# A graph layer's aggregation with the source rows stationary and the destinations moving

## The reference

```
gnn  = segment_sum((xn @ W)[src] * edge_weight, dst)       # 42500 edges
mix  = s * v / s, v = xn @ Wv.T + bv, s per head and row from exp maps of q and k
x1   = x + gnn + mix
r    = layernorm(x1)
out  = x1 + down(silu(gate(r)) * up(r))
```

## Time and profile before

| | |
|---|---|
| profiled execution | 1668.56 us |
| its span, first to last instruction | 1666.6 us |
| PE (matmul) busy | 1643.1 us, 99% |
| DVE busy | 1115.9 us, 67% |
| ACT busy | 487.1 us, 29% |
| POOL busy | 636.8 us, 38% |
| mean granted TensorE clock | 0.998 |
| moved by DMA | 302.89 MB |

### The profile page before, as it was taken

One profiled execution on the slowest core, in us unless ns is written; L12 is line 12 of the kernel. 1 busy time (PEld: TensorE's weight loads), 2 busy tenths in 40 slices (PEclk: granted clock), 3 DMA queues, 4 the chain that ended last, 5 costly groups with the idle time before them and its releaser, 6 DMA issues.

```text
span 1666.6 us, 22401 instructions
## 1 busy us (share of the span) xinstructions
PE 1643.1 (99%) x7896; PEld 1333.1 (80%) x7896; DVE 1115.9 (67%) x2568; ACT 487.1 (29%) x591; POOL 636.8 (38%) x497
## 2 busy tenths in 40 slices
PE   7999999999999999999999999999999999999998
PEld 6899999877777888887788878878777877777665
DVE  7866583576777766755555566676775674774885
ACT  4632311322111111123311023333333232332554
POOL 2011465777777777776688304410300000000000
PEclk9999999999999999999999999999999999999999
DMA  9999888765686755567866656555555345433554
GB/s 314 350 418 347 310 262 252 187 141 122 151 210 146 196 146 131 136 150 176 236 135 136 148 157 198 178 170 162 139 171 138 113 121 136 138 113 93 148 172 124
DMA packets 154777, 302.89 MB, mean 182 GB/s; under 512 B 61624, under 2 KB 92392, under 8 KB 154713
## 3 DMA queue, kind: packets, MB, share of 16 engines
q1 hardware_dynamic: 78469, 206.81, 39.5%
q0 software_dynamic: 66192, 62.07, 17.1%
q10 hardware_dynamic: 10052, 33.26, 6.6%
HBM read 202.88 MB, written 99.20 MB: 181 GB/s over the span
## 4 chain that ended last, share of the span: by engine, by line
PE 85%; DVE 7%; DMA 5%; SPq 1%; issue 1%; ACT 1%; DVEq 0%; ACTq 0%
PE PS L377 21%; PE PS L378 21%; PE PS L379 21%; PE PS L1543 5%; PE PS L1545 5%; PE PS L1544 5%; PE PS L1794 4%; DMA Aside<-A_dense 3%; PE PS L1824 2%; PE PS L1609 2%; DVE SL L1310 1%; DVE stats L1337 1%; DVE zr L1331 1%; DVE AL L1312 1%; DMA z<-zx 1%
## 5 line engine op out<-in xcount | busy, mean ns | idle before, releaser
L726 POOL DMA_INDIRECT A_dense<-wtot,cell x333 | 532.7, 1600 | 213.3 <-DMA A_dense<-wtot,cell 121.2
L377 PE MATMUL PS<-SL,AH 125*125 125x512 f32 x784 | 309.0, 394 | 3.5 <-DVE AL L1312 3.4
L378 PE MATMUL PS<-SH,AL 125*125 125x512 f32 x784 | 310.3, 396 | 0.0
L379 PE MATMUL PS<-SH,AH 125*125 125x512 f32 x784 | 310.1, 396 | 0.0
L377 PE MATMUL PS<-WL,xtH 128*125 128x512 f32 x640 | 251.9, 394 | 0.9 <-DVE xtL L1199 0.8
L378 PE MATMUL PS<-WH,xtL 128*125 128x512 f32 x640 | 251.5, 393 | 0.0
L379 PE MATMUL PS<-WH,xtH 128*125 128x512 f32 x640 | 251.3, 393 | 0.0
L1310 DVE TENSOR_TENSOR SL<-S,SH 125x1024 fp32r<-125x1024 f32 x98 | 119.6, 1221 | 137.6 <-ACT SH L954 137.6
L954 ACT ACTIVATE SH<-S 125x1024 fp32r<-125x1024 f32 (+1 forms) x98 | 104.1, 1062 | 346.1 <-PE PS L379 345.9
L377 PEld LDWEIGHTS PS<-SL,AH 125*125 125x125 f32 x784 | 145.8, 186 | 44.0 <-DVE AL L1312 6.8
L378 PEld LDWEIGHTS PS<-SH,AL 125*125 125x125 f32 x784 | 146.1, 186 | 36.3
(11 more groups left out here) (191 smaller groups left out, 2606.2 us busy)
## 6 DMA issues: line engine op xcount, KB each, us to landing
A_dense<-zeros POOLq DMA_DIRECT2D x40, 1280.0 KB
xt<-xnT SPq DMA_DIRECT2D x60, 500.0 KB
Araw<-A_dense SPq DMA_DIRECT2D x100, 250.0 KB, 2.7
Aside<-A_dense SPq DMA_DIRECT2D x100, 250.0 KB, 3.0
keyrow<-key_rows SPq DMA_DIRECT2D x42, 512.0 KB
ewrow<-weight_rows SPq DMA_DIRECT2D x42, 512.0 KB
xnT<-XT ACTq DMA_DIRECT2D x20, 500.0 KB, 8.2
zx<-in_x SPq DMA_DIRECT2D x20, 448.0 KB
```

Source lines behind the costliest of these rows:

```text
L377: nc.tensor.matmul(o, lh, rl, start=start, stop=False)
L378: nc.tensor.matmul(o, ll, rh, start=False, stop=False)
L379: return nc.tensor.matmul(o, lh, rh, start=False, stop=stop)
L726: pool.indirect_dma_start(cells[m], bass.IndirectOffsetOnAxis(cell[:, col:col + 1], 0), wtot[:, col:col + 1], None, compute_op=ALU.add).th ...
```

## The change

PE's operands in the aggregation change places. Before, 125 destinations of A were stationary and 512 features of S moved. After, a slice of 128 features of S is stationary and the group's 500 destinations move; PSUM holds features on partitions, one slice a bank. DVE no longer adds z: it transposes the banks in blocks of 32 x 32 into an SBUF tensor (`turn_sums`), and POOL adds that to z in device memory by accumulating DMAs (`add_sums`) and loads the sums back into zr (`rows_back`). So that a block row comes out contiguous, ACT writes S with its columns permuted (`sources_out`). r goes away; z takes its place. Statistics move to pairs 3 and 4, rounding to pairs 5 to 8, the last three weight chunks to pairs 1, 2 and 9 of group 1. In the feed-forward stage the last rows' statistics move to tiles 4 and 5, and their rounding to tiles 7, 9, 11 and 13.

```
-ROUNDED_AT = (4, 6, 9, 12)
+ROUNDED_AT = (7, 9, 11, 13)
+STATS_AT = 4
-CHUNK_OF = {(0, h): h - 1 for h in range(1, HALF)} | {(1, h): h + 2 for h in range(3 + GT, HALF)}
+CHUNK_OF = {(0, h): h - 1 for h in range(1, HALF)} | {(1, 1): 9, (1, 2): 10, (1, 9): 11}
+STATS_PAIR, QUANT_PAIR = 3, 5
+FULL_BLOCKS, LAST_ROWS = GN // 32, GN % 32
...
 PE
+        def by_slice(i, sh, sl, d, first, last_one):
+            for k in range(2 * d, 2 * d + 2):
+                cols = slice(k * P, (k + 1) * P)
+                last = product3(PS[:, k, 0:GN], sh[:, cols], sl[:, cols], AH[i][0:ROWS, :], AL[i][0:ROWS, :], first, last_one)
+            return last
...
-                rows = slice(d * ROWS, (d + 1) * ROWS)
-                for c in range(2):
-                    cols = slice(c * 512, (c + 1) * 512)
-                    last = product3(PS[0:ROWS, 2 * d + c, :], AH[i][0:ROWS, rows], AL[i][0:ROWS, rows],
-                                    sh[:, cols], sl[:, cols], first, last_one)
+                last = by_slice(i, sh, sl, d, first, last_one)
...
 DVE
-        def add_z(g):
-            dve.wait_ge(s_zin, 32 * GT + g * 32)
+        def turn_sums(g):
             for d in ORDER:
...
-                nc.vector.tensor_tensor(zr[0:ROWS, d, :], two_banks(d)[0:ROWS], zr[0:ROWS, d, :], ALU.add).then_inc(s_r[d], 1)
+                nc.vector.transpose(sums_of(g)[:, :, 64 * d:64 * d + 64].rearrange("p c (b i) -> p b c i", b=2),
+                                    PS[:, 2 * d:2 * d + 2, :].rearrange("p b (c j) -> p b c j", j=32)).then_inc(s_r[d], 1)
...
         def row_stats(g, tiles):
             for d in tiles:
-                dve.wait_ge(s_r[d], g + 1)
+                dve.wait_ge(s_back, g * (16 * GT) + 16 * (d + 1))
...
+        def group(g, chunks=False, at_end=False):
+            for h in range(HALF):
+                m = g * HALF + h
+                low_of_sources(2 * h, 0, m)
+                sum_of_blocks(1, m)
+                if h == 0:
+                    turn_sums(g - 1)
+                if h == QUANT_PAIR:
+                    inverse_deviation(g - 1)
+                d = h - QUANT_PAIR
+                if 0 <= d < GT:
+                    largest_r(g - 1, d)
...
+                low_of_sources(2 * h + 1, 1, m)
+                if not at_end or h + 1 < HALF:
+                    sum_of_blocks(0, m + 1)
+                if h in (STATS_PAIR, STATS_PAIR + 1):
+                    row_stats(g - 1, ((0, 1), (2, 3))[h - STATS_PAIR])
+                if h == STATS_PAIR + 1:
+                    row_moments(g - 1)
+                if 0 <= d < GT:
+                    round_r(g - 1, d)
...
 DVE, feed-forward stage
-        add_z(GROUPS - 1)
-        row_stats(GROUPS - 1, ORDER[:2])
+        turn_sums(GROUPS - 1)
...
-        row_stats(GROUPS - 1, ORDER[2:])
-        row_moments(GROUPS - 1)
...
-            if t == 2:
+            if t == STATS_AT:
+                row_stats(GROUPS - 1, (0, 1))
+            if t == STATS_AT + 1:
+                row_stats(GROUPS - 1, (2, 3))
+                row_moments(GROUPS - 1)
+            if t == STATS_AT + 2:
                 inverse_deviation(GROUPS - 1)
...
 POOL
+        def add_sums(g, n, blocks):
+            first, last = n * 8, min(n * 8 + 8, FULL_BLOCKS)
+            for a in blocks:
+                cols = slice(a * 256, (a + 1) * 256)
+                pool.dma_start(z_d[g * GN + first * 32:g * GN + last * 32, cols].rearrange("(c j) f -> j c f", j=32),
+                               sums_of(g)[a * 32:(a + 1) * 32, first:last, :], accum_op=ALU.add).then_inc(s_added, 16)
+                if n:
+                    pool.dma_start(z_d[g * GN + last * 32:(g + 1) * GN, cols],
+                                   sums_of(g)[a * 32:a * 32 + LAST_ROWS, last, :], accum_op=ALU.add).then_inc(s_added, 16)
+
+        def rows_back(g, d):
+            if g or d:
+                pool.wait_ge(s_back, 16 * (g * GT + d))
+            if g:
+                pool.wait_ge(s_c5, (g - 1) * GT + d + 1)
+            pool.dma_start(zr[0:ROWS, d, :], z_d[g * GN + d * ROWS:g * GN + (d + 1) * ROWS, :]).then_inc(s_back, 16)
+
+        def residual_rows(g):
+            m, done = (g + 1) * HALF, 192 * g
+            for d in range(GT):
+                pool.wait_ge(s_r[d], g + 1)
+            add_sums(g, 0, (0, 1))
+            pool.wait_ge(s_pe5[0], m + 1)
+            add_sums(g, 0, (2, 3))
+            pool.wait_ge(s_pe5[1], m + 1)
+            pool.wait_ge(s_added, done + 64)
+            add_sums(g, 1, (0, 1))
+            pool.wait_ge(s_pe5[0], m + 2)
+            add_sums(g, 1, (2, 3))
+            rows_back(g, 0)
+            pool.wait_ge(s_pe5[1], m + 2)
+            rows_back(g, 1)
+            pool.wait_ge(s_pe5[0], m + 3)
+            pool.wait_ge(s_added, done + 192)
+            rows_back(g, 2)
+            pool.wait_ge(s_pe5[1], m + 3)
+            rows_back(g, 3)
+
+        for c in range(9):
+            move_chunk(c)
+        residual_rows(0)
+        for c in range(9, 12):
+            move_chunk(c)
...
+        add_sums(GROUPS - 1, 0, range(4))
+        pool.wait_ge(s_added, done + 64)
+        add_sums(GROUPS - 1, 1, range(4))
+        for d in range(GT):
+            if d == 2:
+                pool.wait_ge(s_added, done + 192)
+            rows_back(GROUPS - 1, d)
...
 ACT
         def sources_out(h, i):
...
-            nc.scalar.activation(S[0:ROWS, bass.ds(h * 2 + i, 1), :].rearrange("p o n -> p (o n)"),
-                                 two_banks(i)[0:ROWS], ACT.Copy).then_inc(s_supev[i], 1)
+            nc.scalar.activation(S[0:ROWS, bass.ds(h * 2 + i, 1), :].rearrange("p o (k a i) -> p (o k) a i", k=KT, a=4),
+                                 two_banks(i)[0:ROWS].rearrange("p (a k i) -> p k a i", a=4, k=KT),
+                                 ACT.Copy).then_inc(s_supev[i], 1)
...
+                if h == STATS_PAIR + 1:
+                    deviation(g - 1)
...
-            if t == 1:
+            if t == STATS_AT + 1:
                 deviation(GROUPS - 1)
```

More of the change, by code:

```diff
@@ L254, in layer_kernel, with sums_of @@
     fin = s6("fin", [P, 2, D])
+    last_sums = s6("last_sums", [P, 16, D // 4])
+    def sums_of(g):
+        return last_sums if isinstance(g, int) and g == GROUPS - 1 else sums_in
     PS = nc.alloc_psum_tensor("PS", [P, 8, 512], F32)
@@ L277, in layer_kernel @@
     s_Azero = sems("s_Azero", 2)
[L278 removed]
+    s_acc = {d: sem(f"s_acc{d}") for d in (0, 2, 3)}
     s_bd = sem("s_bd")
@@ L762, in _, with move_chunk @@
             load_chunk(c)
-        for c in range(12):
+        def move_chunk(c):
             if c + 2 < 12:
@@ L978, in high_beside_chunk @@
         def high_beside_chunk(g, h):
-            high_of_pair(g, h)
+            high_of_sources(h * 2, 0, g * HALF + h)
+            d = h - QUANT_PAIR - 1
+            if g and d >= 0:
+                integers(g - 1, d)
+            high_of_sources(h * 2 + 1, 1, g * HALF + h)
             if (g, h) in CHUNK_OF:
@@ L1426, in _ @@
-        group(1)
-        for h in range(3 + GT - 1, HALF):
-            if (1, h) in CHUNK_OF:
-                low_beside_chunk(1, h)
-            else:
-                low_of_pair(1, h)
+            low_of_sources(2 * h, 0, h)
+            sum_of_blocks(1, h)
+            round_chunk(CHUNK_OF[0, h])
+            low_of_sources(2 * h + 1, 1, h)
+            sum_of_blocks(0, h + 1)
+            turn_chunk(CHUNK_OF[0, h])
+        def group(g, chunks=False, at_end=False):
[10 more added lines that the diff above has]
+                    largest_r(g - 1, d)
+                if chunks and (g, h) in CHUNK_OF:
+                    round_chunk(CHUNK_OF[g, h])
+                low_of_sources(2 * h + 1, 1, m)
[7 more added lines that the diff above has]
+                    round_r(g - 1, d)
+                if chunks and (g, h) in CHUNK_OF:
+                    turn_chunk(CHUNK_OF[g, h])
@@ L1432, in _ @@
+        group(1, chunks=True)
         with dve.Fori(2, GROUPS - 1) as g:
             group(g)
-            with dve.Fori(2 + GT, HALF) as h:
-                low_of_pair(g, h)
-        group(GROUPS - 1)
-        with dve.Fori(2 + GT, HALF - 1) as h:
-            low_of_pair(GROUPS - 1, h)
-        low_of_pair(GROUPS - 1, HALF - 1, True)
+        group(GROUPS - 1, at_end=True)
         def scales_back(tiles):
@@ L1761, in first_sources @@
             for d in tiles:
-                rows = slice(d * ROWS, (d + 1) * ROWS)
-                for c in range(2):
-                    cols = slice(c * 512, (c + 1) * 512)
-                    last = product3(PS[0:ROWS, 2 * d + c, :], AH[i][0:ROWS, rows], AL[i][0:ROWS, rows],
-                                    sh[:, cols], sl[:, cols], i == 0, False)
+                last = by_slice(i, sh, sl, d, i == 0, False)
             return last
```

102 lines of the change are left out of this document (33 added, 69 removed).

## The result

The changed kernel runs in 1671.93 us (median of 19 runs, 1666.94 to 1676.10), the kernel before in 1668.33 us beside it (19 runs, 1665.66 to 1671.81): ratio 1.0023, 95% interval 1.0014 to 1.0031. It is slower by 3.6 us. The forecast was 1658.5 and 1668 the upper end of its range: 13.4 us off, on the other side of the kernel before.

A forecast was written before the change was run, and what follows sets the result against it. PE, busy 99% of the span, was taken as the bound, the aggregation priced by its matmul pitch: 1668.56 - 12.6 (columns) + 1.5 (feed-forward statistics) + 1.0 (last row loads) = 1658.5 us, range 1653.5 to 1668.

The forecast's parts named there:

- The matmuls: Aggregation: 2400 matmuls of 500 instead of 512 columns, 5.25 ns less each, 12.6 us gained (12.2 to 13.0).
- rival E: More gained: no statistics stall; second half: 13.0 us from columns, 1.7 us of AL waits after group 0 go; 1654, chance 0.12.
- rival D: Aggregation matmuls: 128 stationary columns or the 500-wide output take back 5 ns, columns bring nothing; 1671 us, chance 0.05.
- The drain: Group's end on DVE: four transposes out of PSUM replace four additions, 1.24 us against 1.22 each, no cost.
- Rival C: Group's end: transposes from PSUM take two passes, 2.5 us each, 4.3 us in each of four groups; 1678.5, chance 0.06.
- The sums' way to memory: POOL's additions (landing 4 us) and row loads: no cost in the groups, 1.0 us (0 to 3) in feed-forward.
- b: Time of one row load on POOL from issue to landing, taken as 4.5 us.
- Rival B: Row loads very late, stalling rows 2 and 3 at pair 4 and feed-forward tile 5; 1676 us, chance 0.07.
- 4b - 30.9: Price in us of late row loads in each of four groups, with b the time of one load.
- 4b - 25.3: Price in us of late row loads at the end, in feed-forward, with b the time of one load.
- Rival A: Row loads of 125 rows go over five engines and land somewhat late, b = 6.7; 1660 to 1663 us, chance 0.20.
- Feed-forward, the rest: Feed-forward: PE loses 1.7 us at tile 6, 1.5 more than before; the rounding steps' later slips (0.6) cost nothing.

The follow-up runs named there:

- the new order: Against the changed kernel with its four row loads no longer waiting for one another: row loads 0 and 1 issued before the second half's additions; 1655.68 us, ratio 0.9920.
- The row loads that depend on nothing: Against the changed kernel: row loads read input x instead of z and are issued ahead of the additions, leaving the sums out; 1653.44 us, ratio 0.9919.

## Why the prediction was wrong, point by point

**The matmuls: mechanism right, size low.** Predicted 226.6 ns and 12.6 us (12.2 to 13.0). Measured 225.7 over an undisturbed group (108.33 us / 480), 6.2 ns less than 231.9: 14.9 us for 2400. A group of before also took 0.6 us more than 480 x 231.9 ns = 111.3, and with that gone in each of the five, 3 us, it comes near the 18.5 above. Those 0.6 us are one or two short waits for AL in each group: after group 0 before has five of them, 1.6 us in all, and none is left with the new order. This is rival E's second half, and it held. The bounds excluded both, because I took the worth of a column from one pair of widths and stretched it no further, and put the waits for AL in a rival. The excess over 512/2.4 shrank too, from 18.6 to 17.4 ns. 128 stationary columns cost nothing that shows beside this; rival D fell.

**The drain: right.** The turned blocks out of PSUM take 1.21 us, the last group's 1.25, against 1.24 taken. PE does not stand at a group's first banks. Rival C fell.

**The sums' way to memory: this step failed.** It said "I bound its landing by 1.8 and 8.5 us, the ends of the 32 KB stores' landings, and take 4", and b = 4.5, the landing of a load with no additions before it. The additions landed in 3.9 to 13.7 us, and b was not one number: 4.2 to 6.1 us for a load with nothing before it (7.7 and 9.6 beside a weight load), 10.5 to 16.1 for the first, behind eight additions. Worse than the number was how I used it. I gave the additions' landing to the chain in one place (1545 to 1549), and treated the row load behind the second eight as if they were not in its way: 1554 + 4b has no term for their drain. The order in which GpSimd issues was in the diff and should have made me add it. Counted from the stage's start, the first row load was issued after 17.0 us instead of 12.8 (1554 - 1541.2), and the four took 32.3 us instead of 18: 16.1 for the first and some 5.4 for each of the others. So the fourth was in after 49.3 us instead of 30.8, 11 us later than the 38.1 at which I had said DVE wants it. And the prediction never asked when rows 0 and 1 are wanted at tile 4, where PE's wait of 7.4 us came from. In the groups the same step failed, and the rest of the working held: 52.3 and 52.9 us are 3.8 and 4.4 past the 48.5 at which row 3 is wanted, less 1 us to spare, and PE waited 2.65 and 3.68.

**Rival B came nearest, with chance 0.07.** It named one place rightly (rows 2 and 3 at pair 4) and half of the other (tile 5; the larger wait was rows 0 and 1 at tile 4). "Against: the median is 4.5" was the error: a median over loads without additions before them says nothing on a load behind eight of them. Its price took one b for all loads and groups. The means were 7.7, 7.9, 6.5, 6.5 and 8.1 at the end, so 4b - 30.9 gives nothing in groups 1, 3 and 4 and 0.5 in group 2, and 4b - 25.3 gives 7.0: 7.5 of the 25.2 us lost. What it lacks is that the first load is issued later (3 us in the groups, 4.2 at the end), rows 0 and 1, and the clock. That its 1676 meets the 1676.1 of the profiled run is chance. "No cost" for the weight chunks that move behind the row loads was not safe either: beside them A's blocks came late in two of the runs above.

**Rival A: wrong.** The Trainium skill ("DMA: Bandwidth & Descriptors", section Why a DMA increments its semaphore by 16 and not by 1) would have let 125 rows go over five engines. Cutting them into 112 and 13 changed the time by less than its uncertainty, and a load of 125 rows (500 KB) with nothing before it lands in 4.2 us and up, like the 4.5 of the 128-partition loads (512 KB) before. Whether that is the page's exception for some POOL copies, no run shows.

**The clock: not priced at all.** After gaps of 2.65 and 3.68 us PE ran 8 and 14 matmuls at half pitch, 1.7 and 2.7 us; in the feed-forward stage the low level cost 4.1 us. Of the 25.2 us that the profiled run lost (4.4 + 6.7 + 14.1) a third, 8.5, is the clock after the gaps.

**Feed-forward, the rest: right.** The row loads that depend on nothing show DVE's load at tiles 4 and 5 by itself, since no row is late there: PE waits 0.79 us for hq and 0.70 for hqT at tile 6, 1.5 together, where 1.7 was predicted. No wait follows up to tile 13, so the drift of tiles 7 to 13 cost nothing, as said.

**The sum as it was:** 1668.56 - 18.5 (columns) + 11.1 (groups 1 and 2) + 14.1 (feed-forward) + 1.15 (later start) = 1676.4, against 1676.1 of the profiled run; the median is 4.2 us lower.

## What to carry to other kernels

Price a transfer by what is queued before it, not by its median on an idle queue: issue what needs only part of the earlier data ahead of the rest, and let nothing urgent be issued behind a burst. Before cutting a chain of serial transfers, ask what they hold back, since the same bytes sooner can make another queue's transfers late. Look also for the rare large transfer that shares the engines with a tight chain: here one stood beside each of the two groups that stalled, and none beside the others. A stall of 2 to 4 us on PE costs more than its length here, because the granted clock falls after it.

## What the runs showed of the hardware that was not expected

- Four accumulating transfers of 256 KB in 1 KB pieces, on GpSimd's queue, were in so far that the next transfer, which waits for them, went out 10.4 us after the first (1536.79 to 1547.22); as plain stores, 7.6 (1528.67 to 1536.22). Accumulating takes 9.3 us more of all 16 engines per 2 MB.
- The recorded issue gets longer as the queue fills: eight additions one behind the other take 1.0, 1.25, 1.75 up to 3.45 us each, plain stores 0.53 to 0.62 throughout. The additions' issues overlap: they start 0.5 to 0.7 us apart all the same.
- A load of 250 KB on SP's queue took up to 15.8 us to land, with 1 MB of weights issued ahead of it and a burst on GpSimd's queue beside it; the maximum in this stretch was 8.9 before and 7.7 after.
- A first row load behind eight additions landed 2.8 to 3.5 us after the last of them, in all five places of after, whether that took 10.5 us in all or 16.1.
- The matmul of 500 columns starts every 225.7 ns, that of 512 every 231.9: 0.52 ns a column between these two, more than the 0.42 between 386 and 512 in the Gram stage.
